# A gated delta-rule attention on one core: 64x64 products of neighbouring units interleaved, the first steps of the block inversion one unit ahead

## The reference

```
x = x + 0.5 * ffn(layernorm(x))
x = x + attention(layernorm(x))
x = x + 0.5 * ffn(layernorm(x))

# attention, for each value head; q, k, v from a projection, a causal convolution of 4 taps and silu
def step(state, inp):
    qt, kt, vt, gt, bt = inp
    state = state * jnp.exp(gt)[..., None, None]
    pred = jnp.einsum('bhk,bhkv->bhv', kt, state)
    delta = (vt - pred) * bt[..., None]
    state = state + kt[..., None] * delta[..., None, :]
    out = jnp.einsum('bhk,bhkv->bhv', qt, state)
# then a norm over each head, a gate silu(z), and W_out
```

## Time and profile before

| | |
|---|---|
| three runs | 3223.53, 3226.09 and 3227.19 us, median 3226.09 |
| profiled execution | 3226.4 us |
| its span, first to last instruction | 3224.7 us |
| mean granted clock of TensorE | 0.928 |
| busy | PE 86%, PEld 63%, DVE 60%, ACT 43%, POOL 21% of the span |

### The profile page before, as it was taken

How to read it: one execution, slowest core, us unless ns; L and a number is a source line. 1 busy time by engine, 2 the same in 40 slices (tenths; PEclk the granted TensorE clock), 3 DMA queues, 4 the chain that set the end, 5 groups by cost and what they waited for, 6 DMA issues and landing times. The chain is left out here.

```text
span 3224.7 us, 58916 instructions
## 1 busy us (share of the span) xinstructions
PE 2757.1 (86%) x19218; PEld 2040.5 (63%) x19219; DVE 1943.3 (60%) x3720; ACT 1380.5 (43%) x4437; POOL 671.4 (21%) x959
## 2 busy tenths in 40 slices
PE   2699992556999999999999999999999983699992
PEld 2366661433677777777777777777777772366661
DVE  3122223478898898798798898898886544122222
ACT  0111110233566666566566566666665550111110
POOL 3100004132122222222222222222221112200003
PEclk7799996677999999999999999999999996799996
DMA  5122201145544544544544544545543312122202
GB/s 183 44 94 95 96 26 57 48 149 159 171 141 148 169 151 140 166 152 136 169 152 136 172 150 144 168 146 161 151 130 102 104 46 90 48 95 90 98 27 85
DMA packets 371258, 385.86 MB, mean 120 GB/s; under 512 B 214980, under 2 KB 285508, under 8 KB 371012
## 3 DMA queue, kind: packets, MB, share of 16 engines
q1 hardware_dynamic: 356420, 321.82, 32.6%
q0 software_dynamic: 14592, 60.83, 5.4%
HBM read 239.03 MB, written 143.52 MB: 119 GB/s over the span
## 5 line engine op out<-in xcount | busy, mean ns | idle before, releaser
L480 PE MATMUL f_ps_up<-f_wbuf,f_xgT 128*128 x1248 | 499.1, 543 | 5.4 <-issue 3.4
L575 DVE TENSOR_TENSOR f_h<-f_h,f_ps_up 128x448 f32<-128x448 f32 x156 | 97.0, 621 | 555.0 <-ACT f_h L549 555.0
L549 ACT ACTIVATE f_h<-f_ps_up 128x448 f32<-128x448 f32 x156 | 84.8, 544 | 635.0 <-PE f_ps_up L480 635.0
L480 PEld LDWEIGHTS f_ps_up<-f_wbuf,f_xgT 128*128 128x128 f32 x1248 | 231.2, 192 | 189.1 <-issue 184.8
L1156 PE MATMUL at_bank<-xnT,at_w_qk 128*128 128x512 f32 x512 | 273.9, 664 | 63.6 <-DVE at_qk L1467 57.6
L1467 DVE SCALAR_TENSOR_TENSOR at_qk<-at_bank,at_taps_qk,at_qk 128x510 f32<-128x510 f32 (+2 forms) x384 | 285.0, 744 | 60.9 <-ACT at_qk L1341 51.5
L1467 DVE SCALAR_TENSOR_TENSOR at_vT<-at_bank,at_taps_v,at_vT 128x510 f32<-128x510 f32 (+2 forms) x384 | 280.6, 744 | 36.4 <-ACT at_vT L1348 27.3
L1321 PE MATMUL at_bank<-at_w_out,at_yT 128*128 128x256 f32 x1024 | 260.1, 399 | 37.8 <-issue 31.5
L502 PE MATMUL f_ps_y<-f_wbuf,f_hT 128*128 x1092 | 248.8, 380 | 1.6 <-DVE f_hT L579 1.6
L1169 PE MATMUL at_bank<-xnT,at_w_vz 128*128 128x512 f32 x512 | 235.1, 602 | 15.6 <-DVE at_qk L1467 11.9
L1727 POOL TENSOR_SCALAR at_small<-at_small 128x4 f32<-128x4 f32 x64 | 18.3, 285 | 1089.2 <-ACT at_squares L1375 1089.2
(11 more groups left out here) (216 smaller groups left out, 5570.4 us busy)
## 6 DMA issues: line engine op xcount, KB each, us to landing
f_wbuf<-in_L_ffn_w_dram POOLq DMA_DIRECT2D x48, 896.0 KB, 8.0
at_steps_e<-steps_kept SPq DMA_DIRECT2D x64, 512.0 KB, 6.0
pt_kept<-at_pt_made SPq DMA_DIRECT2D x64, 512.0 KB, 3.1
mt_kept<-at_mt_made SPq DMA_DIRECT2D x64, 512.0 KB, 4.5
at_mt<-mt_kept SPq DMA_DIRECT2D x64, 512.0 KB, 5.1
at_pt<-pt_kept SPq DMA_DIRECT2D x64, 512.0 KB, 4.8
qk_kept<-at_qk SPq DMA_DIRECT2D x64, 256.0 KB, 3.0
ks_kept<-at_ks_made SPq DMA_DIRECT2D x64, 256.0 KB, 2.1
```

Source lines behind the costliest of these rows:

```text
L480: last = te.matmul(ps_up[hf][w][:, 0:MH], xgT[b][:, k, :], wbuf[:, bass.ds(off + (w * WSIZE + k * M + hf * MH), MH)], start=(k == 0), stop ...
L575: v.tensor_tensor(part, part, ps_up[hf][1][:, 0:MH], ALU.mult).then_inc(h_ready, 1)
```

## The change

- Stages: `inv_x` and `inv_n` work one unit further ahead than `inv_last` (stage 1 against 0), and all that feeds them moves with them: the largest stage grows from 11 to 12, so `walk` runs over 79 iterations and not 78.
- `inv_x` 64 of a unit and `inv_last` of the unit before are issued product by product in turns, the one on rows 0 to 63 into partitions 64 to 127 of one bank, the other on rows 64 to 127 into partitions 0 to 63 of the other bank. `inv_last` by itself is left for the last unit only.
- `invT` has three buffers, not two; `xb` is split into `xb32` and `xb64`.
- `diag_b` goes: GpSimd writes the diagonal into `decay`, and the scan reads and writes `decay`. The waits for the mixes of the previous unit go from `scan` to `diag`.
- All order tuples are new.

```
 STAGE = {
-    "load_qk": 11, "proj_qk": 11, "conv_qk": 11, "gate_qk": 11,
+    "load_qk": 12, "proj_qk": 12, "conv_qk": 12, "gate_qk": 12,
...
-    "blocks_in": 6, "blocks": 5, "low": 5,
-    "blocks_out": 1, "load_c": 1, "load_t": 1,
+    "blocks_in": 7,
+    "blocks": 6, "low": 6,
+    "blocks_out": 2, "load_c": 2, "load_t": 2,
...
-    "load_d": 0, "inv_x": 0, "inv_n": 0, "inv_last": 0,
+    "inv_x": 1, "inv_n": 1,
+    "load_d": 0, "inv_last": 0,
...
-ACT_ORDER = (("weigh", 0), ("conv_qk", 0), ("copy_state",), ("conv_qk", 1), ("y_copy", 0), ("from_state",),
+ACT_ORDER = (("weigh", 0), ("norm",), ("copy_state",), ("conv_qk", 0), ("inv_n",), ("y_copy", 0), ("conv_qk", 1),
...
-POOL_ORDER = (("scales",), ("diag",), ("out_weights",), ("low",), ("norm_scale",))
+POOL_ORDER = (("scales",), ("diag",), ("out_weights",), ("norm_scale",), ("low",))
...
                 def load_t(u):
                     sp.wait_ge(s["blocks_stored"], 32 * (u[0] + 1))
-                    at_least(sp, s["u_psum"], 2 * (idx(u) - 1))
+                    at_least(sp, s["u_psum"], 2 * (idx(u) - 2))
...
+                def last_of(u, n):
+                    return te.matmul(inv_bank[1][0:64, 64 * n:64 * n + 64], xb64[64:P, n, :], invT[idx(u) % 3][64:P, n, 64:P],
+                                     start=True, stop=True)
...
+                    pe.wait_ge(s["n_copied"], idx(u) + 1)
+                    pe.wait_ge(s["n_copied_t"], idx(u) + 1)
+                    at_least(pe, s["x_ready"], 2 * idx(u))
+                    for n in range(N8):
+                        if idx(u):
+                            last = last_of(shift(u, -1), n)
+                            if n == N8 - 1:
+                                last.then_inc(s["last_psum"], 1)
+                        x64 = te.matmul(inv_bank[0][64:P, 64 * n:64 * n + 64], m[0:64, n, 64:P], w[0:64, n, :], start=True, stop=True)
+                    x64.then_inc(s["x_psum"], 1)
...
                 def inv_last(u):
+                    if idx(u) < UNITS - 1:
+                        return
...
-                    at_least(dve, s["mt_ready"], idx(u))
-                    at_least(dve, s["pt_ready"], idx(u))
                     v_.tensor_tensor_scan(decay[:].rearrange("p n m -> p (n m)"), steps_e[:],
-                                          diag_b[:].rearrange("p n m -> p (n m)"), 0.0, ALU.mult, ALU.add).then_inc(s["decay_ready"], 1)
+                                          decay[:].rearrange("p n m -> p (n m)"), 0.0, ALU.mult, ALU.add).then_inc(s["decay_ready"], 1)
...
                     dve.wait_ge(s["x_psum"], 2 * idx(u) + (1 if b == 32 else 2))
+                    if b == 64:
+                        at_least(dve, s["last_psum"], idx(u))
...
-                    at_least(pool, s["decay_ready"], idx(u))
+                    at_least(pool, s["mt_ready"], idx(u))
+                    at_least(pool, s["pt_ready"], idx(u))
```

More of the change, by code:

```diff
@@ L859 @@
-DRAIN_POOL_ORDER = (("norm_scale",), ("scales",), ("low",), ("diag",), ("out_weights",))
+FILL_SP_ORDER = (("blocks_out",), ("load_wo",), ("load_t",), ("load_vz",), ("load_steps",), ("blocks_in",),
+                 ("load_d",), ("load_qk",), ("load_c",), ("spill",))
+FILL_PE_ORDER = (("proj_qk", 0), ("proj_qk", 1), ("state",), ("project", 0), ("on_state", 0), ("proj_v", 2),
+                 ("project", 1), ("z", 0), ("on_state", 1), ("products", 0), ("y_turn", 0), ("turn", 1), ("inv_n",),
+                 ("inv_x", 32), ("solve", 0), ("y_turn", 1), ("proj_v", 3), ("turns", 0), ("inv_last",),
+                 ("output", 0), ("turn", 0), ("inv_x", 64), ("solve", 1), ("z", 1), ("products", 1), ("output", 1),
+                 ("turns", 1))
@@ new lines @@
+FILL_POOL_ORDER = (("norm_scale",), ("scales",), ("diag",), ("low",), ("out_weights",))
+SP_ORDER = (("load_wo",), ("blocks_out",), ("load_c",), ("load_d",), ("load_steps",), ("load_t",), ("blocks_in",),
+            ("spill",), ("load_qk",), ("load_vz",))
+PE_ORDER = (("inv_x", 32), ("solve", 0), ("proj_qk", 0), ("state",), ("inv_n",), ("proj_qk", 1), ("y_turn", 0),
+            ("on_state", 0), ("on_state", 1), ("inv_x", 64), ("turn", 1), ("y_turn", 1), ("project", 0), ("turn", 0),
+            ("project", 1), ("proj_v", 2), ("proj_v", 3), ("solve", 1), ("inv_last",), ("products", 0),
+            ("products", 1), ("z", 0), ("turns", 0), ("z", 1), ("turns", 1), ("output", 0), ("output", 1))
```

133 lines of the change are left out of this document (59 added, 74 removed).

## The result

The changed kernel takes 3198.69 us (median of 4 runs, 3198.25 to 3204.51), the kernel before 3224.81 us in the same series (3223.12 to 3227.19): ratio 0.992, 95% interval 0.9904 to 0.9936. It is faster by 26 us. The forecast was 3148, with 3105 to 3205 as its range: the direction was right and the time lies in the range, but two thirds of the gain are missing, and one term, that of the head change, has the wrong sign.

What follows compares the result with a forecast made beforehand. TensorE was taken as the bound, busy throughout quiet iterations, with a longer iteration at each head change. The terms -60 + 15 - 45 + 12 = -78 on 3226.4 us gave 3148 us, range 3105 to 3205.

Steps and rivals of the forecast that it cites:

- Part A: TensorE's 64x64 products of two units alternated: 1.04 us saved per unit, -60 us in all.
- Rival 1: The two 64x64 tiles on TensorE do not overlap, so alternation saves nothing: 3208 us, 10%.
- Part B: Steady iterations: VectorE's denser order makes TensorE wait 0.3 us an iteration, +15 us over 52.
- Rival 2: VectorE becomes the bound in the steady iterations, the denser order costing +52 us: 3185 us, 15%.
- Part D: Longer pipe: one more filling and one more draining iteration, one steady less, +12 us.
- Part C: Head change: block store lands 3 us earlier in the iteration, leaving 1.2 of 4.7 us: 13 x -3.5 = -45 us.
- rival 4: Head change gets worse: `low` follows `norm_scale`, store lands 2 us later, 5 us more per head: 3258 us, 8%.
- rival 3: Head-change stall stays, blocks still queued before the convolution and their load beside the store: 3193 us, 15%.
- What was called upsetting: ScalarE's wait for the spill or its inverse copies, placed in slack, standing before the 64x64 group; no size given.

Runs made afterwards that it cites:

- experiment 6: Changed kernel with the qk convolutions ahead of the blocks on VectorE in head iterations, and `low` ahead of `norm_scale` on GpSimd: 3123.43 us, ratio 0.9681.
- experiment 11: As experiment 6, with the second piece of the blocks also behind the qk convolutions in VectorE's heaviest iteration: 3123.45 us, ratio 0.9677.
- experiment 7: Changed kernel with only GpSimd's order put back, `low` ahead of `norm_scale`: 3137.12 us, ratio 0.9721.
- experiment 9: Kernel before the change with only `norm_scale` put ahead of `low` in GpSimd's steady order: 3278.57 us, ratio 1.0161.
- experiment 2: Changed kernel with only the second piece of the blocks moved behind the qk convolutions on VectorE, in every steady iteration: 3176.67 us, ratio 0.983.
- experiment 10: As experiment 7, with the second piece of the blocks behind the qk convolutions in head iterations alone: 3132.70 us, ratio 0.9709.
- experiment 8: The kernel with the head order, with ScalarE's copies of the inverse (`inv_n`) ahead of its first qk convolution: 3152.98 us, ratio 0.977.
- the kernel with the head order: Changed kernel with both qk convolutions before the first two pieces of the blocks, and the fourth behind the mixes, on VectorE in head iterations: 3154.32 us, ratio 0.9766.

## Why the prediction was right and wrong

**What bounds the kernel** was read rightly: quiet iterations with TensorE busy throughout, and a head change of its own.

**Part A was right.** 1.10 us for the alternated group were taken, 1.08 measured. Rival 1 falls (16 records of each line interleaved). The Trainium skill (TensorE: Matmul & The Clock Gate, Part 3: Packing small matmuls) says that a weight load overlaps running matmuls only where the row group differs; the trace agrees so far as these tiles differ in rows and share the 1.08 us, while L1240 and L1241 in the earlier trace rows overlap with the same rows. By its section LDWEIGHTS, 32 such loads one after another would be an estimated 1.7 us; measured are 1.08.

**Part B was too high.** +15 was taken for what the denser order makes late; the quiet iteration fell by 1.01 of the possible 1.04 to 1.06, and the heaviest one is 27.84. Of the 0.66 of wait before the projection in that iteration 0.3 is there (it starts 10.7 us after the first solve, 10.4 in a quiet one), and most of it is made up behind: TensorE is busy for 27.70 of 27.84. Rival 2 (VectorE the bound) falls for this kernel; experiments 6 and 11, where the head stall is gone, only suggest it for one iteration in four.

**Part D was right for the filling** (16.6 for one more iteration and the way to it, 15.9 taken) and Part A was cautious for the drain: its iterations are 1.25 us shorter each, where half of 1.04 was taken. With A and B: forecast -33, measured -55.

**Part C is the step that failed.** It said that the store would land 3 us earlier, leaving 1.2 of the 4.7 us of excess: -45. Measured, VectorE goes on 0.6 us later (+9.9 against +9.3 in the table; the means of 13 are +9.9 and +9.4), 1.1 later counted from the iteration's first product, and the excess is 6.8: +27. That is 72 us between the two, more than the whole miss of 50; A, B and D give 22 back. Three things in its working were wrong:

1. The step took the two weight loads out of the way of the store, and saw that `low` now follows `norm_scale`, but put that into rival 4 as "about 1 us later" and as a mishap of its own, instead of into the sum. From the rows it is 2.4 us of `norm_scale` (1436.20 to 1438.62), and 2.0 more for the second copy, which runs beside VectorE's scan.
2. It reckoned the landing from memory traffic (five DMAs in front of or beside the store; in rival 3 the load of the blocks). But between the four kernels of the table the time of issue makes nearly all the difference, and the way from issue to VectorE 0.8 us at most. The load of the blocks is a neighbour in SyncE's queue: what stands behind it, the spill and the store, can't be issued until GpSimd has finished `low`, though neither needs that load (the store needs `low` itself, the spill doesn't). Experiments 7 and 9 show this from both sides: 61.6 us taken out of the changed kernel by the order of two names, 50 us added to the kernel before by the same swap.
3. It called the second piece of the blocks ahead of the convolution a wash. With the store late it is not: experiment 2 gave 22 us for moving it. With the store in time it is: experiment 10 gave 4 us, within the two intervals.

With `low` first the excess is 1.7 us a head ((1435.5 of steady part less 1413.2) over 13), where the forecast had 1.2, and the time 3137, where it had 3148. So the size that Part C hoped for was about right, and the one move of GpSimd's order cost it all. The reason that it gave is not borne out even there: VectorE goes on 2.9 us earlier than in the kernel before (2.3 from the first product), and 2.1 of it (1.5) is an earlier issue. That the size fits is partly luck. **Rival 4** named the right chain at 8%; its price of 5 us a head was for a store 2 us later than before, and VectorE went on only 0.6 to 1.1 later, since the weight loads had gone from between: from the load of the blocks to the last of the store the issuing takes 7.3 us in the changed kernel and 10.0 in the kernel before with `low` last (the table). **Rival 3** (the stall stays, 3193) is nearest in time, but that is luck: the head change cost 27 us more instead of staying as it was, and Parts A, B and D gave 22 more than was taken.

**What was called upsetting**, waits on ScalarE in front of the 64x64 group, is there (9.5 us, 7 times), and by experiment 8 (on the kernel with the head order) costs nothing by itself.

## What to carry to other kernels

On an engine that issues DMAs in order, find for each issue what it waits for, and who stands behind it: one load that waits for a slow, idle-looking engine holds up every later store. GpSimd is busy 21% of the span here, and the order of two of its steps is worth 2% of the kernel. Where a sum has a term for a transfer that comes earlier, work out the time of issue of everything in front of it from the order and the rows, before guessing at traffic. And when a wait has several causes in a row, repair the first: the later ones may turn out to be a wash.

## What the runs showed of the hardware

**A GpSimd copy beside VectorE's scan.** The second copy of `low` takes 2.65 us in 12 of the changed kernel's 16 heads, and 0.62 to 0.65 in the other four and in all heads of experiment 7. In the rows of the changed kernel it starts at 1439.19 and ends at 1441.84, while the scan runs from 1438.94 to 1441.40: it ends 0.44 us behind the scan, as if it had been held until then. The scan took 2.46 us where it otherwise takes 2.28; the first copy was still under way when it started. In the kernel before, where the second copy is under way when the scan starts (1463.49 to 1464.11, the scan from 1463.66), the copy takes its usual 0.62 and the scan 2.60, in 12 of its 16 heads: the one that starts first keeps its time. By the Trainium skill (SBUF — State Buffer, Who interferes with whom) a VectorE instruction with two inputs in SBUF contends with a GpSimd instruction that reads SBUF. The trace agrees: the scan reads `steps_e` and `decay`, the copy reads `w_up`. The kernel before, with the same swap (experiment 9), has its copies clear of the scan, 0.64 and 0.65 us, and pays for the order alone (with GpSimd's wait for ScalarE in it).

**Two 64x64 tiles.** Alternated they cost as much as one (1.08 us for 32 records, 1.07 for 16); side by side without alternation, 1.82.

**The clock.** In the changed kernel it is granted at 0.50, the 1.2 GHz level, for 68 us of the steady part, in 12 of its 13 head iterations after TensorE has stood idle there; in the kernel before for 48. In experiment 7 it is at that level once, for 3.4 us, in a head iteration of 32.2 us, and at 1.00 in the others, 29.0 to 30.3 us long. Part of each head's excess is this: a gap of 2.6 us before the projection stands in an iteration that is 7.7 us longer than a quiet one (how much of it is the clock, no run separates).
